# Twelve-row operands of a linear-attention normalizer laid out over 128 partitions

## The reference

```
x = x + gnn(xn) + mix(xn)          # gnn: two graph attention layers over 21250 edges
x = x + ffn(layernorm(x))          # ffn: router, two of four experts, 768 -> 1536 -> 768
mix: y = x + linear_attention(ln(x)); y + gelu(ln(y) @ fc1 + b1) @ fc2 + b2     # 768 -> 3072 -> 768
```

```
q = elu(q) + 1.0;  k = elu(k) + 1.0
kv = einsum('bhsd,bhse->bhde', k, v)
z = 1.0 / einsum('bhsd,bhd->bhs', q, k.sum(axis=-2))
out = einsum('bhde,bhsd,bhs->bhse', kv, q, z)
```

## Time and profile before

| | us |
|---|---|
| median of 3 runs | 1955.73 |
| lowest, highest | 1953.89, 1957.2 |
| profiled execution, first to last instruction (span) | 1953.0 |
| TensorE busy in the span | 1900.2 |
| VectorE busy | 1171.0 |
| ScalarE busy | 609.8 |
| GpSimd busy | 401.0 |

### The profile page before, as it was taken

One profiled execution on the slowest core, in us unless ns is written; L12 is line 12 of the kernel. 1 busy time (PEld: TensorE's weight loads), 2 busy tenths in 40 slices (PEclk: granted clock), 3 DMA queues, 4 the chain that ended last, 5 costly groups with the idle time before them and its releaser, 6 DMA issues.

```text
span 1953.0 us, 28486 instructions
## 1 busy us (share of the span) xinstructions
PE 1900.2 (97%) x10981; PEld 1811.5 (93%) x10981; DVE 1171.0 (60%) x2102; ACT 609.8 (31%) x1182; POOL 401.0 (21%) x311
## 2 busy tenths in 40 slices
PE   7999999999899999999999999999999999999998
PEld 4677999999799999789999999999989999999998
DVE  8998678998894323778524435254557435274348
ACT  6533238787784412225200001010330101010013
POOL 1000002210001222214413314043023404043130
PEclk9999999999899999999999999999989999999999
DMA  6332402121245110033201102020231102021014
GB/s 177 112 119 86 116 14 57 43 60 54 68 139 144 57 49 9 17 103 112 65 9 57 46 20 59 7 65 17 80 97 49 50 17 73 1 81 40 26 50 125
DMA packets 80943, 125.53 MB, mean 64 GB/s; under 512 B 7334, under 2 KB 51656, under 8 KB 80814
## 3 DMA queue, kind: packets, MB, share of 16 engines
q1 hardware_dynamic: 76254, 110.47, 19.5%
q10 hardware_dynamic: 4560, 13.31, 2.3%
HBM read 98.30 MB, written 25.45 MB: 63 GB/s over the span
## 4 chain that ended last, share of the span: by engine, by line
PE 86%; DVE 6%; ACT 5%; issue 3%; ACTq 0%; DVEq 0%; SPq 0%; DMA 0%
PE pb L1135 25%; PE pa L679 25%; PE pb L679 10%; PE pa L745 5%; PE pa L891 3%; PE pb L811 3%; PE pb L1044 3%; PE pa L845 3%; PE pb L891 2%; ACT sm L1557 1%; PE pb L687 1%; PE pb L922 1%; ACT o1h L1583 1%; PE pa L1006 1%; DVE sm L2146 1%
## 5 line engine op out<-in xcount | busy, mean ns | idle before, releaser
L1813 ACT ACTIVATE tr<-pb,V 128x418 f32<-128x418 f32 (+1 forms) x144 | 87.6, 610 | 765.9 <-PE pb L1135 752.9
L1135 PE MATMUL pb<-X_hi,uw_hi 128*128 128x416 f32 (+1 forms) x864 | 305.5, 354 | 2.4 <-DVE uw_lo L2464 2.4
L1135 PE MATMUL pb<-X_hi,uw_lo 128*128 128x416 f32 (+1 forms) x864 | 304.9, 353 | 0.0
L1135 PE MATMUL pb<-X_lo,uw_hi 128*128 128x416 f32 (+1 forms) x864 | 304.8, 353 | 0.0
L679 PE MATMUL pa<-dw_hi,hh 128*125 128x384 f32 x960 | 246.9, 338 | 1.0 <-ACT tr L1813 0.7
L679 PE MATMUL pa<-dw_hi,hl 128*125 128x384 f32 x960 | 246.3, 338 | 0.0
L679 PE MATMUL pa<-dw_lo,hh 128*125 128x384 f32 x960 | 246.1, 337 | 0.0
L2411 DVE CAST hh<-tr 128x418 fp32r<-128x418 f32 (+1 forms) x144 | 115.0, 799 | 202.4 <-ACT tr L1813 202.4
L1289 POOL CAST uw_hi<-raw 128x768 fp32r<-128x768 f32 x47 | 42.7, 908 | 715.4 <-PE pb L1135 618.3
L679 PEld LDWEIGHTS pa<-dw_hi,hh 128*125 128x125 f32 x960 | 172.4, 186 | 2.0 <-ACT tr L1813 1.0
L679 PEld LDWEIGHTS pa<-dw_hi,hl 128*125 128x125 f32 x960 | 173.1, 186 | 0.0
(11 more groups left out here) (418 smaller groups left out, 3517.1 us busy)
## 6 DMA issues: line engine op xcount, KB each, us to landing
raw<-in_L_mix_fc_w SPq DMA_DIRECT2D x48, 384.0 KB, 3.3
raw<-in_L_ffn_w SPq DMA_DIRECT2D x47, 384.0 KB, 3.2
md<-md_d SPq DMA_DIRECT2D x11, 546.9 KB
md_d<-mds SPq DMA_DIRECT2D x10, 546.9 KB
raw<-in_L_mix_qkv_w SPq DMA_DIRECT2D x24, 192.0 KB, 4.3
md<-md_d ACTq DMA_DIRECT2D x8, 546.9 KB
TOK<-in_x SPq DMA_DIRECT2D x10, 336.0 KB
xn_d<-TOK SPq DMA_DIRECT2D x10, 336.0 KB
```

The source lines that it names most:

```text
L1135: last = nc.tensor.matmul(pb[:, j % 4, 0:n], w_[:, kk, :], x_[:, kk, o:o + n], start=(kk == 0 and q == 0), stop=(kk == KT - 1 and q == 2))
L1813: last = A_(RE[f"tr{j % 3}"][:, 0:w], pb[:, j % 4, 0:w], ACT.Identity if func == "mish" else func, bias=bias(b))
```

## The change

The selector and the four `z` tiles get 128 partitions instead of 12. The rows from 12 up hold zeros: those of the selector because `zf` is cleared and selected over 128 rows, those of the `z` tiles because GpSimd clears the tiles once, ahead of the query stage. VectorE still writes twelve rows. The scratch `zf` moves from `sm0` to `c0w`, and with it the wait for `zsel_ok` from ScalarE to VectorE.

```diff
-        zsel = sb("zsel", [NHEAD, KT, P], f32r)
+        zsel = sb("zsel", [P, KT, P], f32r)
...
-                  + [("zr", [NHEAD, CH], fp32)] + [(f"z_{k}{q}", [NHEAD, CH], f32r) for q in range(2) for k in ("hi", "lo")]
+                  + [("zr", [NHEAD, CH], fp32)] + [(f"z_{k}{q}", [P, CH], f32r) for q in range(2) for k in ("hi", "lo")]
...
                 pe.wait_ge(*at("z_ok", c + 1))
+                if r == 0:
+                    pe.wait_ge(*at("z_zero", 4))
                 for n, z_ in enumerate((RE[f"z_hi{c % 2}"], RE[f"z_lo{c % 2}"])):
...
-            zf = RW["sm0"][0:NHEAD, 0:D].rearrange("p (m a n) -> p m a n", m=KT, a=2)
+            zf = RE["c0w"][:].rearrange("p (m a n) -> p m a n", m=KT, a=2)
...
                 split_page(kv_page(1, k), kvw[1][k])
+            for q in range(2):
+                for k in ("hi", "lo"):
+                    last = g_.memset(RE[f"z_{k}{q}"][:].bitcast(fp32), 0.0)
+                    last.then_inc(sem("z_zero"), 1)
             pool.wait_ge(*at("kv_mm", NT))
...
-            act.wait_ge(*at("zsel_ok", 1))
             for k in range(3):
                 page_high(PG_WU + k, wu[k][0], func=ACT.Copy)
...
                 if k == 0:
+                    dve.wait_ge(*at("zsel_ok", 1))
                     v.tensor_scalar(RE["c0w"][:], raw[i % NRAW][:], vcol("gnn_norm_b", k), None, ALU.mult).then_inc(sem("c0_w"), 1)
...
-                zr, zh, zl = RE["zr"][:, 0:w], RE[f"z_hi{c % 2}"][:, 0:w], RE[f"z_lo{c % 2}"][:, 0:w]
+                zr, zh, zl = RE["zr"][:, 0:w], RE[f"z_hi{c % 2}"][0:NHEAD, 0:w], RE[f"z_lo{c % 2}"][0:NHEAD, 0:w]
                 dve.wait_ge(*at("q_den", KT * (c + 1)))
+                dve.wait_ge(*at("z_zero", 4))
```

## The result

| | before | changed |
|---|---|---|
| median of 5 runs beside each other, us | 1954.68 | 1944.99 |
| lowest, highest | 1953.85, 1957.2 | 1943.56, 1947.67 |
| span of the profiled execution | 1953.0 | 1942.9 |
| mean clock granted to TensorE in it | 0.991 | 0.993 |

The ratio is 0.9948 [0.9936, 0.9961]. The traces of this pair show two parts: steps near the predicted sum, and two stretches of low clock that are gone.

A forecast was written before the change was run, and what follows sets the result against it. TensorE, busy for 97% of the span, was taken to bound the kernel. Savings by call, 0.30 + 3.20 + 0.20 + 0.40 + 2.25 = 6.35 us, took 1955.73 to 1949.4 us; the range was 1946.5 to 1952.6.

The forecast's parts named there:

- The steps: TensorE's height changes around the `z` pairs of 18 `q_apply` calls: 0.40 us per call in dense rounds, 6.35 us in all.
- the wait for `TK`: TensorE's one wait after the stage for a projection's sum, 0.3 us: said to move along with TensorE's transposes, no gain counted.
- calls 1 to 8: `q_apply` calls in query-stage rounds with no wait: 8 x 0.40 = 3.20 us saved.
- Its signs: Changed trace: `z` matmuls 128x416 at 350 ns, starts 0.19 us apart, loads not beginning with their matmuls except after waits, rounds 4.93 us.
- Call 0: First `q_apply`, behind a 2.5 us wait: 0.30 us saved, 0.10 between the pair and 0.20 on the way out.
- the way out of call 9 and all of call 10: Before `q_sum(17)`: 0.60 us of savings fall into TensorE's idle time, worth nothing; that stretch grows from 2.0 to 2.4 us.
- Nobody late next: VectorE's `z_lo` of the third chunk and `attended(11)` have 2.5 and 1.5 us slack, losing 0.4 and 0.8: nothing becomes late.
- The first rival: Shorter rounds wait for VectorE; calls 1 to 8 give half, gain some 3.5 us: 1952.2 us, chance 0.12.
- The second rival: Rows are not what costs; the `z` pair's gap has another reason (bank, operand): gain 0, 1955.7 us, chance 0.07.
- Clears and start: Four GpSimd clears, 1.6 to 2.6 us, hidden in 27.18 idle; ScalarE's wait at the start taken as 0 of 0 to 0.4.
- The step from span to time: Whole time against the profiled span: the median was 2.7 us above it, and the same 2.7 was added after the change.
- the term of the clock: 1.2 GHz stretches behind both idle stretches stay; rival of one fewer (1948.0 us) or more (1950.8), 1.4 us each, chance 0.06.

The follow-up runs named there:

- e10_warm_before: Kernel before plus unread 128-row matmuls in TensorE's two idle stretches, 13 ahead of the wait for `z_ok`, 10 ahead of that for `q_lo(17)`: median 1950.14 us, ratio 0.9974.
- e11_warm_after: Changed kernel plus the same unread matmuls, 13 and 10, in TensorE's two idle stretches of the query stage: median 1945.1 us, ratio 0.9945.
- after_third: The changed kernel run again without an edit, on the same chip as three other kernels: median 1945.49 us, ratio 0.9957.
- e7_rows12: Changed kernel with all its other edits, but every `z` pair reads only the 12 used rows: median 1953.36 us, ratio 0.9998.
- e3_idle12: Changed kernel, but the `z` pairs of calls 0 and 9 to 11, beside the idle stretches, read 12 rows: median 1949.29 us, ratio 0.9969.
- e8_idle12_again: The kernel with 12 rows in calls 0 and 9 to 11 alone, run again without an edit: median 1949.81 us, ratio 0.9972.
- e12_gap_tall: Changed kernel, but `z` pairs read 128 rows only in calls 0, 1 and 8 to 11, and 12 rows elsewhere: median 1951.74 us, ratio 0.9976.
- e4_rows64: Changed kernel, but every `z` pair reads 64 of the 128 rows: median 1953.07 us, ratio 0.9991.
- e1_rows96: Changed kernel, but every `z` pair reads 96 of the 128 rows: median 1946.93 us, ratio 0.9956.

## Why the prediction was wrong, and where it was right

- **The steps were right in kind and nearly in size, their exact sum by luck.** Predicted 6.35 us; between e10_warm_before and e11_warm_after the calls give 5.8, and 0.5 come from the wait for `TK`, of which the prediction said "it moves along", a term put at nothing. For calls 1 to 8 the mechanism holds to 0.1 us. Its signs came: 128x416 and 350 ns, 0.19 us apart, loads ahead of their matmuls, rounds of 4.93 us. Call 0 gave 0.18 instead of 0.30, since the step inside its pair stayed at 0.30. That the way out of call 9 and all of call 10 are worth nothing shows in the idle stretch that grew (2.3 us; 2.4 forecast).
- **Nobody late next: right for calls 1 to 8, wrong in one place.** The first rival (VectorE takes half of their gain back) is refuted: their rounds take 4.93 us. But `q_apply(13)` now starts with the end of `attended(11)`, where the prediction had 0.7 us of slack left. The steps around it, 0.37 and 0.30 us in the first changed trace, 0.49 and 0.29 in e11_warm_after, take back 0.3 to 0.4 us. In after_third there was a wait of 0.9 us for `X_lo` besides, behind an `X_hi` of 2.06 us.
- **Rows are what costs: right.** The second rival (the gap belongs to the pair for another reason) is refuted by e7_rows12 against the changed kernel. Its page of the Trainium skill, TensorE: Matmul & The Clock Gate, Why this matters for your kernels, has a single matmul of K=32 take the time of K=128. The traces agree for one matmul without a change of height (349 ns), and not for a stream that alternates: 12 and 64 rows both cost 0.40 us a pair.
- **Clears and start: right.** 1.6 us of clears, hidden (forecast 1.6 to 2.6). ScalarE's wait was taken as 0 of 0 to 0.4 us, and no gain from it is shown. The step from span to time was not as assumed: the prediction took 2.7 us for both kernels; 1.7 were measured before and 2.1 after the change.
- **The step that failed is the term of the clock.** The sum had it at nothing: the prediction said "Both idle stretches stay, one grows", let both falls of the clock stay with them, and gave a fall more or fewer a chance of 0.06. The idle stretches did stay. But a fall behind them isn't a fixed term of a kernel: it came in some executions and not in others, of the same kernel. In the profiled pair both falls are gone, and the stage's 9.54 us are 6.35 of steps and waits (e10_warm_before less e11_warm_after), 3.03 for the two falls (124.36 - 121.33) and 0.16 left over. On the means the changed kernel is 9.5 us faster, 3.1 more than the sum, and its low clock takes 14.35 +- 0.50 us by the measure above, for 17.97 +- 0.25 before. The sum thus lacked a term of about 3 us, and the low end of the range took one fall at 1.4 us where about two were needed. The price of one was right: 1.2 to 1.5 us measured.
- **What shows that cause, and what stays open.** The unread matmuls take the idle stretches away and leave the steps; they give before 4.9 us and the changed kernel 0.6. So it is shown that the rest of the gain hangs on these two idle stretches, and for the profiled pair that it is the falls behind them. That all of the rest is falls is not shown for the means: of the 4.9 us the traces explain 3.0. Why the changed kernel has fewer falls is not shown either. Height beside the idle stretches is supported by e3_idle12, e8_idle12_again and e12_gap_tall on the mean, and left in doubt by e7_rows12, e4_rows64 and e1_rows96. That short rows are needed for a fall is refuted by e1_rows96 and after_third.

## What to carry to other kernels

Operands with few rows inside a stream of 128-row matmuls cost more than their own length shows, here 0.40 us a pair: read the distances from start to start, and lay them out over 96 partitions or more with zero rows if something idle can clear them (64 did not help here). Where TensorE waits 2 us in a dense stretch, price the low clock behind the wait as a term that can go or come with any change beside it, and let the range hold all such falls. Independent work, or even matmuls that nobody reads, can be issued ahead of the wait; here that was worth 4.9 us in one kernel and 0.6 in the other. And a sum that is met exactly should still be followed call by call.

## What was unexpected of the hardware

- 64 rows cost as much as 12 (0.28 to 0.30 us from start to start), 96 as little as 128 (0.19 us). The step inside a short pair is 0.29 us too, though no height changes there; no run shows why.
- Idle stretches of 2.0 to 2.5 us were followed by 3.4 us at 1.2 GHz in some executions of one program, by 6.8 us in others, and by nothing in others still. The engine had been dense before them.
- 23 matmuls without a reader made a kernel faster by 4.9 us.
- A clear on GpSimd: 0.74 us for 128x768, 0.73 for 12x768, 0.45 for 128x418.
